# Inverse row sums copied to their heads' partitions by DMA instead of by matmuls, in a cross-attention kernel

## What is computed

```python
q = _split_heads(hidden_states @ Wq.T, H)
k = _split_heads(text @ Wk.T, H)
v = _split_heads(text @ Wv.T, H)
out_text = _merge_heads(_attend(q, k, v, sm_scale))      # softmax(q k^T * sm_scale) v
k_ip = _split_heads(ip @ Wk_ip.T, H)
v_ip = _split_heads(ip @ Wv_ip.T, H)
out_ip = _merge_heads(_attend(q, k_ip, v_ip, sm_scale))
out = out_text + IP_SCALE * out_ip
out = out @ Wo.T + bo
return out + residual                                    # residual = hidden_states
```

## Time and profile before

| | |
|---|---|
| time, median of 3 runs | 714.61 us (714.51 to 715.17) |
| span of the profiled execution | 712.9 us |
| PE busy | 679.8 us, 95% |
| ACT busy | 493.3 us, 69% |
| DVE busy | 441.4 us, 62% |
| POOL busy | 224.0 us, 31% |
| DMA | 57.44 MB, the queue's packets took 26.0% of 16 engines' span |

### The profile page before, as it was taken

The page is one execution under the profiler, slowest core; times in us unless marked ns, Lnnn a source line. Parts: engine busy times, 40 slices in busy tenths (PEclk is TensorE's granted clock), DMA queues, the critical chain, the costliest instruction groups (busy, mean ns, idle before and its releaser), DMA issues.

```text
span 712.9 us, 18904 instructions
## 1 busy us (share of the span) xinstructions
PE 679.8 (95%) x6514; PEld 560.9 (79%) x6514; DVE 441.4 (62%) x956; ACT 493.3 (69%) x1078; POOL 224.0 (31%) x261
## 2 busy tenths in 40 slices
PE   8959789999999999999999999999999999999997
PEld 8958566777877788778877887888778877887777
DVE  5786667665757565665656565655657575756633
ACT  3984687876767676767776777677767776776641
POOL 4020103243423324242424233242434233242333
PEclk9989899999999999999999999999999999999999
DMA  8940021313131312222121312112131313111211
GB/s 321 408 191 16 17 62 33 83 48 94 51 91 46 92 50 77 58 56 86 52 82 52 90 52 82 52 56 86 46 95 47 89 46 95 51 51 47 61 47 66
DMA packets 34690, 57.44 MB, mean 81 GB/s; under 512 B 4832, under 2 KB 27232, under 8 KB 34400
## 3 DMA queue, kind: packets, MB, share of 16 engines
q1 hardware_dynamic: 34656, 56.99, 26.0%
HBM read 35.34 MB, written 10.49 MB: 64 GB/s over the span
## 4 chain that ended last, share of the span: by engine, by line
PE 53%; ACT 30%; issue 10%; DVE 6%; ACTq 1%; POOL 0%; DVEq 0%
PE pv_ps L780 11%; ACT q_stack L397 9%; PE q_ps L711 9%; ACT probs L405 8%; PE x_ps L711 7%; PE b_ps L752 7%; PE a_ps L735 7%; PE x_ps L789 5%; PE sum_ps L769 5%; ACT y L428 3%; ACT q_hi L390 3%; ACT pv_sb L410 2%; ACT attn_hi L434 1%; DVE k_stack L631 1%; DVE k_stack L641 1%
## 5 line engine op out<-in xcount | busy, mean ns | idle before, releaser
L405 ACT ACTIVATE probs<-b_ps 77x512 f32<-77x512 f32 x320 | 181.1, 591 | 153.3 <-PE b_ps L752 151.7
L571 DVE TENSOR_REDUCE row_max<-a_ps 128x4 f32<-128x308 f32 x320 | 138.5, 474 | 86.6 <-PE a_ps L735 84.0
L562 DVE TENSOR_TENSOR q_stack<-q_ps,q_hi 32x256 fp32r<-32x256 f32 x320 | 134.3, 420 | 36.0 <-ACT q_hi L390 32.3
L397 ACT ACTIVATE q_stack<-q_hi 32x256 fp32r<-32x256 f32 x320 | 133.0, 416 | 10.0
L352 POOL TENSOR_TENSOR attn_lo<-scaled,attn_hi 128x256 fp32r<-128x256 f32 x80 | 58.9, 737 | 182.3 <-ACT attn_hi L434 182.3
L752 PE MATMUL b_ps<-q_stack,k_stack 98*77 98x256 f32 x640 | 115.6, 282 | 0.6 <-ACT probs L405 0.5
L735 PE MATMUL a_ps<-k_diag,q_hi 128*128 128x308 f32 x320 | 93.7, 333 | 7.5 <-DVE row_max L571 7.5
L598 DVE TENSOR_TENSOR scaled<-x_ps,pv_sb 128x512 f32<-128x512 f32 x75 | 51.9, 692 | 68.2 <-PE x_ps L789 67.6
L358 POOL TENSOR_TENSOR res<-y,res 128x256 f32<-128x256 f32 x70 | 51.1, 730 | 136.7 <-ACT y L428 136.7
L347 POOL TENSOR_TENSOR scaled<-scaled 128x256 f32<-128x256 f32 x80 | 58.5, 732 | 102.6 <-DVE scaled L598 102.5
L752 PEld LDWEIGHTS b_ps<-q_stack,k_stack 98*77 98x77 f32 x640 | 85.7, 147 | 2.3 <-ACT probs L405 1.3
(11 more groups left out here) (111 smaller groups left out, 939.3 us busy)
## 6 DMA issues: line engine op xcount, KB each, us to landing
x_raw<-x_in SPq DMA_DIRECT2D x16, 640.0 KB, 4.1
q_stack<-q_stack SPq DMA_DIRECT2D x80, 128.0 KB, 2.3
res<-x_in SPq DMA_DIRECT2D x75, 128.0 KB, 2.1
y_out<-res SPq DMA_DIRECT2D x75, 128.0 KB, 1.7
stage<-wk_in SPq DMA_DIRECT2D x6, 640.0 KB, 8.2
stage<-wv_in SPq DMA_DIRECT2D x6, 640.0 KB, 10.3
wq_raw<-wq_in SPq DMA_DIRECT2D x1, 1600.0 KB, 9.3
wo_raw<-wo_in SPq DMA_DIRECT2D x1, 1600.0 KB, 14.7
```

What stands on the lines that cost most here:

```text
L397: done = nc.scalar.activation(q_stack[0:D, u.slot, j, :], q_hi[j * D:(j + 1) * D, u.slot, :].bitcast(F32), ACT.Copy)
L405: nc.scalar.activation(probs[0:KEYS, j, :], b_ps[j % 2][0:KEYS, :], ACT.Exp).then_inc(b_drained, 1)
L562: done = nc.vector.tensor_tensor(q_stack[D:2 * D, u.slot, j, :], q_ps[rows, 0:N], q_hi[rows, u.slot, :].bitcast(F32), ALU.subtract)
L571: nc.vector.tensor_reduce(row_max[:, u.slot, br, :, sub], bank[:, 0:BLK].rearrange("p (j n) -> p j n", j=GROUP), AXIS.X, ALU.max).then_inc ...
```

## The change

`spread`, `low_rows`, `inv_hi` and `inv_parts` go, with the instructions on POOL and DVE that made them, and so do all spread matmuls. `inv` holds the plain inverses. SP issues for each unit two DMAs, one for each branch, from eight rows of `inv` (every 16th), each repeated 16 times, to the 128 partitions of a new tile `inv_spread`, which has two slots. `normalise` multiplies `inv_spread[:, slot]` by `pv_sb[:, g]`.

The waits change with it. SP waits for `scaled_done` of the slot's last user (g > 0) or for `inv_done` (g = 0). `normalise` waits for `inv_landed`. `keep_sums` waits until the copies of the tile before have landed. `project_out` waits for `y_done` of the chunk before. On SP the copies of a unit with g > 0 stand first in `emit`, for unit u-5, and those for g = 0 last. On DVE `normalise` for g = 0 moves behind `max_turned`. ACT and POOL keep their order.

```diff
@@ -149,8 +146,7 @@
         attn_lo = sbuf("attn_lo", [P, BATCHES, GROUPS, N], F32R)
         res = sbuf("res", [P, GROUPS, N])
         inv = sbuf("inv", [P, N])
-        inv_hi = sbuf("inv_hi", [P, N], F32R)
-        inv_parts = sbuf("inv_parts", [P, N], F32R)
+        inv_spread = sbuf("inv_spread", [P, 2, BRANCHES * N])
         y = sbuf("y", [P, 2, N])
 
         v_chan = [stage[0][:, (GROUP + 2) * BRANCHES * N + br * GROUPS * BATCHES * KEYS:][:, 0:GROUPS * BATCHES * KEYS]
@@ -290,8 +285,22 @@
                 sp.dma_start(q_stack[2 * D:3 * D, u.slot].bitcast(F32),
                              q_stack[0:D, u.slot].bitcast(F32)).then_inc(q_third[u.slot], DMA)
 
+            def spread_inverse(u):
+
+                if u.g == 0:
+                    wait(sp, inv_done, u.tile(1, 1))
+                else:
+                    wait(sp, scaled_done, u.number(1, -1))
+                for br in range(BRANCHES):
+                    row = BRANCHES * u.g + br
+                    sp.dma_start(inv_spread[:, u.slot, br * N:(br + 1) * N],
+                                 inv[row::HALF, :].unsqueeze(1).broadcast_to([P // HALF, HALF, N])
+                                 ).then_inc(inv_landed[u.slot], DMA)
+
             def emit(u):
-                ahead = u.tile_plus(2)
+                ahead, norm = u.tile_plus(2), u.plus(-SPREAD_LAG)
+                if norm.exists() and norm.g > 0:
+                    spread_inverse(norm)
                 if u.plus(1).exists():
                     maxima(u.plus(1))
                 if u.plus(2).exists():
@@ -303,12 +312,16 @@
                 if u.g == 2 and ahead.exists():
                     wait(sp, x_lo_done, u.tile(1, 2))
                     sp.dma_start(x_raw[:], x_d[ahead.t, ahead.batch]).then_inc(x_loaded, DMA)
+                if norm.exists() and norm.g == 0:
+                    spread_inverse(norm)
 
             third_block(Unit(0, 0))
             maxima(Unit(0, 0))
             third_block(Unit(0, 1))
             emit.engine = sp
             stages(emit)
+            for g in range(GROUPS):
+                spread_inverse(LAST.plus(g))
             for n, c in enumerate(LAST_CHUNKS):
                 sp.wait_ge(last_added, n + 1)
                 sp.dma_start(out_d[c.t, c.batch, :, c.g, :], last_place(c)).then_inc(stored, DMA)
@@ -418,7 +425,12 @@
             def keep_sums(u):
 
                 wait(act, pv_ready, u.number(1, GROUPS))
-                wait(act, inv_done, u.tile(INV_STEPS))
+                before = u.tile_plus(-1)
+                if before.exists():
+                    last = before.plus(GROUPS - 1)
+                    wait(act, inv_landed[last.slot], last.uses_of_slot(SPREAD_DMAS))
+                    previous = before.plus(GROUPS - 2)
+                    wait(act, inv_landed[previous.slot], previous.uses_of_slot(SPREAD_DMAS))
                 nc.scalar.activation(inv[:], sum_ps[:, 0:N], ACT.Copy).then_inc(sums_kept, 1)
 
             def add_bias(c):
@@ -583,19 +592,13 @@
 
                 wait(dve, sums_kept, u.tile(1, 1))
                 nc.vector.reciprocal(inv[:], inv[:]).then_inc(inv_done, 1)
-                wait(dve, inv_spread, u.number())
-                wait(dve, inv_done, u.tile(INV_STEPS, 1))
-                nc.vector.tensor_copy(inv_hi[:], inv[:]).then_inc(inv_done, 1)
-                wait(dve, inv_done, u.tile(INV_STEPS, 2))
-                nc.vector.scalar_tensor_tensor(out=inv_parts[:], in0=inv_hi[:].bitcast(F32), scalar=low_rows[:],
-                                               in1=inv[:], op0=ALU.mult, op1=ALU.add).then_inc(inv_done, 1)
-
-            def normalise(u, bank=x_ps):
-
-                wait(dve, inv_spread, u.number(1, 1))
+
+            def normalise(u):
+
+                wait(dve, inv_landed[u.slot], u.uses_of_slot(SPREAD_DMAS))
                 wait(dve, pv_drained, u.number(1, 1))
                 wait(dve, attn_lo_done, u.number(1, -1))
-                nc.vector.tensor_tensor(scaled[:, u.slot, :], bank[:], pv_sb[:, u.g, :],
+                nc.vector.tensor_tensor(scaled[:, u.slot, :], inv_spread[:, u.slot, :], pv_sb[:, u.g, :],
                                         ALU.mult).then_inc(scaled_done, 1)
 
             def finish_last(n):
@@ -609,12 +612,14 @@
 
             def emit(u):
                 norm, nxt = u.plus(-1 - SPREAD_LAG), u.plus(1)
-                if norm.exists():
+                if norm.exists() and norm.g > 0:
                     normalise(norm)
                 if nxt.exists():
                     for k in range(MAXES):
                         max_piece(nxt, k)
                     max_turned(nxt)
+                if norm.exists() and norm.g == 0:
+                    normalise(norm)
                 if u.g == 0 and u.tile_plus(-1).exists():
                     invert_sums(u.tile_plus(-1))
                 if u.plus(2).exists():
@@ -782,24 +786,9 @@
                                                 probs[:, j, br * N:(br + 1) * N], start=True, stop=True)
                 done.then_inc(pv_ready, 1)
 
-            def spread_matmuls(u, bank):
-
-                for br in range(BRANCHES):
-                    sel = spread[:, BRANCHES * u.g + br].rearrange("p j d -> p (j d)")
-                    done = nc.tensor.matmul(bank[:, br * N:(br + 1) * N], sel, inv_parts[:], start=True, stop=True)
-                done.then_inc(inv_spread, 1)
-
-            def spread_inverse(u):
-
-                if u.g == 0:
-                    wait(pe, inv_done, u.tile(INV_STEPS, INV_STEPS))
-                wait(pe, scaled_done, u.number())
-                wait(pe, y_done, u.number(1, 1 + SPREAD_LAG - OUT_LAG))
-                spread_matmuls(u, x_ps)
-
             def project_out(c):
 
-                wait(pe, scaled_done, c.number(1, OUT_LAG - SPREAD_LAG))
+                wait(pe, y_done, c.number())
                 out_chunk(c, x_ps)
 
             def out_chunk(c, bank):
@@ -894,11 +870,7 @@
                 if chunk.exists():
                     project_out(chunk)
                 row_sums(u)
-                if norm.exists() and norm.g > 0:
-                    spread_inverse(norm)
                 weigh_values(u)
-                if norm.exists() and norm.g == 0:
-                    spread_inverse(norm)
                 if u.fixed and u.number() == OUT_LAG - 1:
                     pe.wait_ge(wo_lo_done, GROUPS)
 
```

Behind the loop, for the last tile, DVE's and PE's parts change so (SP's is the last lines of its hunk above):

```diff
@@ -681,21 +686,20 @@
             for item in range(GROUPS + 2, K_ITEMS, 2):
                 place_v(item)
             dve.wait_ge(bo_loaded, DMA)
-            dve.wait_ge(low_rows_done, 1)
             emit.engine = dve
             stages(emit)
             normalise(LAST.plus(-1))
             invert_sums(LAST)
 
             finish_last(0)
-            normalise(LAST, sum_ps)
+            normalise(LAST)
             for n in (1, 2):
                 finish_last(n)
             for g in (1, 2, 3):
-                normalise(LAST.plus(g), sum_ps)
+                normalise(LAST.plus(g))
                 if g + 2 < GROUPS:
                     finish_last(g + 2)
-            normalise(LAST.plus(4), sum_ps)
+            normalise(LAST.plus(4))
             for n in range(GROUPS, 2 * GROUPS):
                 finish_last(n)
 
@@ -847,7 +828,7 @@
                 def chunk(n):
 
                     if n == 0:
-                        pe.wait_ge(scaled_done, LAST.number())
+                        pe.wait_ge(y_done, LAST_CHUNKS[0].number())
                     elif n == 1:
                         pe.wait_ge(pv_drained, UNITS)
                     else:
@@ -856,23 +837,18 @@
 
                 chunk(0)
                 chunk(1)
-                spread_last(0)
                 chunk(2)
-                spread_last(1)
                 chunk(3)
-                spread_last(2)
                 grow(0)
                 chunk(4)
-                spread_last(3)
                 grow(1)
-                spread_last(4)
                 for k in range(2, GROUPS):
                     grow(k)
 
             def emit(u):
 
 
-                nxt, norm, chunk = u.plus(1), u.plus(-SPREAD_LAG), u.plus(-OUT_LAG)
+                nxt, chunk = u.plus(1), u.plus(-OUT_LAG)
 
                 def find_max(k):
                     if nxt.exists():
```

24 lines of the change are left out of this document (3 added, 21 removed).

## The result

The changed kernel takes 801.04 us (median of 5 runs, 793.97 to 808.69) against 714.61 us: a ratio of 1.118, 95% interval 1.111 to 1.124. The ratio is that of the four runs within 1.5% of the fastest (the fifth, 808.69 us, is not in it). It is 12% slower; 772 us (730 to 792) had been forecast. The profiled execution spans 803.9 us, 91.0 us more than before.

A forecast was written before the change was run, and what follows sets the result against it. PE, busy 95% of the span, was taken as the bound. From 712.9 us: −50.9 spread, +56.3 wait, +34.5 low clock, +15.6 x_raw load, +2 end gave 770.4, as a median 772 us; range 730 to 792.

The forecast's parts named there:

- the low clock after it, in g = 1 and g = 2: PE's clock falls to 1.2 GHz after the row-sum wait, costing 2.3 us per tile beyond it: 34.5 us.
- end: Behind the loop, copies stand openly between the reciprocal and the last tile: +2 us (0 to 5).
- What is removed: Without spread matmuls and their wait, PE's ordinary units fall from 8.05 to 7.25 us: −50.9 us in all.
- The copies for g = 0: Late copies hold DVE's multiplication, then ACT, so PE waits 3.75 us at g = 1 row sums: 56.3 us.
- The load of x_raw: In 13 tiles it delays copies and max_rows behind it; PE's scores wait 1.2 us each: 15.6 us.
- Two inputs in SBUF: DVE's multiplication and POOL exclude each other; hidden at g = 1, otherwise costing up to 13 us.
- The clock holds: Rival: the waits come but PE's clock does not fall; 737 us, chance 0.12.
- The copies use 16 engines: Rival: copies run over 16 DMA engines rather than 8, shortening both waits; 749 us, chance 0.10.
- Faster: Rival: copies for g = 0 land by the end of max_turned, PE waits 1.15 us; 683 us, chance 0.10.
- Worse: Rival: queueing in g = 2 units and DVE held by split_x also show; above 792 us, chance 0.04.

The follow-up runs named there:

- e4: Changed kernel with 36 useless float32r matmuls on PE ahead of the row sums of units with g = 1; 803.19 us, ratio 1.123.
- e6: Changed kernel with 9 useless float32 matmuls on PE ahead of the row sums of units with g = 1; 803.95 us, ratio 1.125.
- e7: Changed kernel with SP's load of x_raw moved behind the copies and max_rows, some 2 us later; 792.59 us, ratio 1.109.
- e1: Changed kernel without its 160 copies, DVE multiplying by 1.0, so the division is left out; 695.25 us, ratio 0.972.
- e5: Changed kernel with copies read from 16 rows of inv, each repeated 8 times (wrong rows); 760.18 us, ratio 1.064.
- e2: Changed kernel with a sixth pv_sb slot and ACT's attn_high for g = 0 moved to its unit's end; 797.86 us, ratio 1.116.
- e12: e10 with the right rows and one 256 KB transfer per unit instead of two of 128 KB; 687.43 us, ratio 0.963.
- e10: e8 with the copies read from 16 rows of inv, as in e5 (wrong rows); 672.98 us, ratio 0.941.
- e8: Changed kernel with more inv_spread and pv_sb slots, copies issued earlier, and DVE, ACT and POOL work for g = 0 reordered; 754.58 us, ratio 1.055.
- e9: Changed kernel with the max_rows transfer issued by ACT behind its fourth exp instead of by SP; 827.33 us, ratio 1.159.
- e11: e10 with the max_rows transfer issued by ACT behind its fourth exp; 693.44 us, ratio 0.971.

## Why the forecast was right and where it was wrong

The direction, the mechanism and its place were right; the size was 33.5 us short on the span (803.9 for 770.4). Term by term, with the means of the table:

| term | forecast | measured |
|---|---|---|
| spread removed | −50.9 | 15 × (39.58 − 5 × 7.24) = −50.7 |
| g = 1, the wait | 56.3 | 15 × 4.65 = 69.8 |
| the low clock after it, in g = 1 and g = 2 | 34.5 | 15 × (1.63 + 0.61) = 33.6 |
| g = 4, behind x_raw | 15.6 | 15 × (9.28 − 7.24) = 30.6 |
| g = 3 and g = 0 | 0 | 15 × (0.28 + 0.01) = 4.4 |
| end | 2 | 3.6 |
| sum | 57.5 | 91.3 |

Two terms failed by their size: the load of `x_raw` by 15 us and the wait for the copies for g = 0 by 13.5 us.

**What is removed** held to 0.2 us.

**The copies for g = 0.** The chain DMA, DVE, keep_pv, fourth exp, PE is there link by link, and the order of ACT was the right thing to look at. The wait was 4.51 us in the unit shown and 4.65 in the mean, and not 3.75, because the multiplication began at +7.25 instead of +6.35. SP's issue isn't the reason: the second copy of the pair goes out at +3.26, where +3.3 was forecast,

```profile
478.29 0.64 SPq L296 DMA_DIRECT2D inv_spread<-inv  x1
```

and is in use 4.0 us later (482.28), where 3.05 was forecast. So it is the landing that was priced too low. The queue's share gives a rate: (0.342 × 803.9 − 0.260 × 712.9) × 16 = 1433 us of engine time for 160 × 128 KB, 0.070 us per KB, where the forecast took 0.056 from two transfers of other kinds. On 8 engines that is an estimate of 1.12 us a copy and not 0.9, which explains about half of the 0.9 us; what makes up the rest (the reload of `res` just ahead, or the second pair right behind) wasn't tried apart.

The clock cost what was forecast: 13.53 − 7.24 − 4.51 = 1.78 us beyond the wait in the unit shown, 1.63 in the mean, and 0.61 more in the next unit, 2.2 in all for a forecast of 2.3. In e4 and e6 it wasn't had back by keeping the clock up: other waits came out that it had covered, besides the gap that the experiment brought.

**The load of x_raw** is the step that failed most, by 15 us. Its mechanism was right, and e7, which moves the load, takes all of the lengthening out of those units. The forecast had one wait of 1.2 us a tile and nothing behind it. The mean wait of 1.3 us bears the 1.2 out, but the waits differ from tile to tile, up to 2.35 us, and behind the four longest of twelve the clock fell: the row at 459.33 has a wait of 2.31 us and 4.0 us of lengthening. So of the 2.04 us a tile 1.3 are the wait and 0.74 what lies beyond it, most of it the low clock, a term that the forecast had for one wait and put at nothing for its neighbour. (The load stands in front in 13 tiles, not 15: 13 × 2.04 = 26.5 us; the table takes 15 throughout, so that its sum is that of the whole.)

**Two inputs in SBUF.** "In the unit that PE has already lost" was right: the collision comes at that unit's end (487.07, 1.59 us beside POOL's 2.90, for 0.69 alone) and PE waits for none of it. So was the warning of what it costs without that cover: in e1 and e6, where PE isn't late, the unit with g = 2 takes 7.96 and 7.95 us for 7.24, with a wait for `row_max` of 0.45 us, inside the forecast's 0.9. That these units take 7.85 us in the changed kernel looks alike and has another cause, the end of the low clock. The collision itself is as in the earlier trace rows and as the Trainium skill (SBUF — State Buffer, "Who interferes with whom") says; by that rule, the trace agrees.

**The rivals.** "The clock holds" is out: 0.50 and 0.57 after the waits. "The copies use 16 engines" is out by the count of packets, and e5, which makes it true, gives 760 us where 749 was worked out. "Faster" turned at 3.4 us per tile of wait and clock; 6.9 came (4.65 + 1.63 + 0.61). "Worse", above 792, is what came, but not for its two reasons: DVE held by split_x cost nothing, and the queueing was in g = 4 and not in g = 2. It had been given 0.04, too little for a case that needed only one term to be a fourth larger and another twice as large. It was also wrong to take the queue's effects one by one: e2 shows a second wait of 2.3 us for `max_rows` standing behind the first, and had the first been less, as in the rival "faster", this one would have come.

## What to carry over

Transfers that wait in one queue delay the smallest one behind them. Before adding 256 KB per unit to a queue, look which transfer on it has the least slack, here 8 KB of maxima, and price the wait behind every place where copies stand ahead of it, by the longest that the rows allow and not the mean alone, since the low clock came behind the long waits only. Look also for the issues that wait for a landing, here the reload of `res` for the store: whatever delays that store delays all that SP issues behind it. In this kernel copies from 16 source rows ran over 16 engines and those from 8 over 8; the same bytes from 16 rows, and issued where nothing urgent is behind, turned +12% into −4% (e12). When two waits have one cause, an experiment that removes one may show nothing (e2); change the cause. And when a unit is longer than the rest, ask for the wait in it before naming an engine: the low clock of one unit can end in the next.

## What was not expected of the hardware

- SP's time to issue one and the same transfer isn't constant. A copy took 589 to 1332 ns in the changed kernel (median 667) and 538 to 623 ns in e10 (median 586), with the same number of copies. `y_out` took 0.36 us in the median of the changed kernel and up to 2.31 us in e8. The bytes that are under way don't decide it: right behind the 640 KB of `x_raw` (452.46) two copies took 1.35 us, and of four in a row with less ahead of them the fourth (479.75) took 1.31. What does wasn't tried.
- Engine time per KB, worked out from the queue's share, hardly depends on the shape of the copy: 0.070 us per KB on 8 engines (0.073 in e8), (0.400 × 672.4 − 0.260 × 712.9) × 16 / 20480 = 0.065 in e10 on 16, and 0.070 in e12 with rows of 2 KB, half as many packets in the copies. What differs is how long a copy stands in the queue.
- Moving one DMA issue of 0.62 us per unit to ACT, which was busy 61% of the time in the changed kernel and 73% in e10, cost 26 us (e9 against the change) and 20 us (e11 against e10). The new place of `max_rows` in ACT's order is part of that; the two weren't tried apart.
